# Opening of a four-stage convolution kernel: order of the sample loads, of sample 2's statistics and of the first stack copies

## The reference

```python
x = x + conv(_gn(x))        # stage 0: 3x3, reflect padding; kernel mixed per sample from 3 experts
x = x + conv1(abs(_gn(x)))  # stage 1: 3x3 depthwise, zero padding
x = x + box(_gn(x))         # stage 2: 17x17 mean, zero padding
x = x + mlp(_gn(x))         # stage 3: sum of the 8 neighbours, then 5 pixelwise layers, elu between
```

## Time and profile before

| | |
|---|---|
| median of 3 runs | 767.77 us (767.4 to 771.08) |
| the profiled execution | 776.6 us, its span 774.7 |
| PE, DVE, ACT, POOL busy | 624.3, 611.5, 563.9, 200.6 us |
| DMA | 85.5 MB, mean 110 GB/s; SP's queue 78.6 MB, ACT's 6.3 |
| chain that ended last | PE 36%, DVE 22%, ACT 17%, DMA 8%, issue 8%, SP's queue 6% |
| first layer of round 1 | starts at 137.91 us |

### The profile page before, as it was taken

The page is one execution under the profiler, slowest core; times in us unless marked ns, Lnnn a source line. Parts: engine busy times, 40 slices in busy tenths (PEclk is TensorE's granted clock), DMA queues, the critical chain, the costliest instruction groups (busy, mean ns, idle before and its releaser), DMA issues.

```text
span 774.7 us, 13144 instructions
## 1 busy us (share of the span) xinstructions
PE 624.3 (81%) x4142; PEld 188.2 (24%) x4142; DVE 611.5 (79%) x1100; ACT 563.9 (73%) x1081; POOL 200.6 (26%) x291
## 2 busy tenths in 40 slices
PE   0351845899798999899889988999899789889992
PEld 0211211223222222233223322322232223222220
DVE  1352785598959998989988998879887889769993
ACT  0112110689868998899889988998898968898882
POOL 1302024402541235213521353125300630230000
PEclk9985886899989999999999999999999999999996
DMA  5759499407985739254834574455640560065002
GB/s 98 139 91 178 101 189 211 73 14 146 170 192 97 173 88 206 66 112 107 183 87 109 110 164 107 109 112 132 141 109 3 125 146 1 2 146 125 1 1 54
DMA packets 72865, 85.53 MB, mean 110 GB/s; under 512 B 8674, under 2 KB 58354, under 8 KB 72818
## 3 DMA queue, kind: packets, MB, share of 16 engines
q1 hardware_dynamic: 68096, 78.58, 47.6%
q10 hardware_dynamic: 4722, 6.34, 4.5%
HBM read 9.14 MB, written 8.39 MB: 23 GB/s over the span
## 4 chain that ended last, share of the span: by engine, by line
PE 36%; DVE 22%; ACT 17%; DMA 8%; issue 8%; SPq 6%; POOL 1%; ACTq 1%; DVEq 0%; POOLq 0%
PE pz L756 19%; PE pc L702 8%; ACT u L610 7%; DVE g L991 6%; ACT u L618 6%; PE pc L733 6%; DMA win<-y 5%; DVE u L987 3%; ACT u L615 2%; DVE bn L923 2%; DVE box_sum L1024 2%; DMA xs<-in_x_dram 2%; DVE xs L974 2%; PE po L763 2%; DMA stack<-near_sum 2%
## 5 line engine op out<-in xcount | busy, mean ns | idle before, releaser
L610 ACT ACTIVATE u<-pz 128x512 f32<-128x512 f32 x472 | 275.4, 603 | 93.3 <-PE pz L756 92.7
L756 PE MATMUL pz<-g,wT 64*64 64x512 f32 x1536 | 296.7, 614 | 18.7 <-DVE g L991 15.1
L991 DVE SCALAR_TENSOR_TENSOR g<-u,pz 128x512 f32<-128x512 f32 x384 | 250.3, 681 | 62.1 <-ACT u L618 58.7
L618 ACT ACTIVATE u<-u 128x512 f32<-128x512 f32 x472 | 289.6, 643 | 1.3
L756 PEld LDWEIGHTS pz<-g,wT 64*64 64x64 f32 x1536 | 80.5, 132 | 212.2 <-issue 210.4
L733 PE MATMUL pc<-win,t 64*32 64x512 f32 x1392 | 98.0, 667 | 27.0 <-DMA win<-y 16.0
L702 PE MATMUL pc<-box_sum,box_mat 128*128 128x512 f32 x180 | 90.9, 621 | 12.3 <-DVE box_sum L1024 12.3
L923 DVE BATCH_NORM_STATS2 bn<-xs 128x6 f32<-128x512 f32 (+1 forms) x128 | 82.8, 682 | 22.0 <-DMA xs<-in_x_dram 20.2
L468 POOL TENSOR_TENSOR stat<-stat,con 128x1 f32<-128x1 f32 x32 | 22.5, 704 | 272.9 <-DVE stat L943 272.9
L991 DVE SCALAR_TENSOR_TENSOR g_last<-u,pz 128x512 f32<-128x512 f32 x128 | 82.5, 680 | 9.1 <-ACT u L618 7.1
L756 PE MATMUL pz<-stack,wT 64*64 64x512 f32 x512 | 81.7, 620 | 9.5 <-DMA stack<-near_sum 4.2
(11 more groups left out here) (87 smaller groups left out, 366.6 us busy)
## 6 DMA issues: line engine op xcount, KB each, us to landing
stack<-near_sum SPq DMA_DIRECT2D x90, 192.0 KB, 4.0
win<-y SPq DMA_DIRECT2D x56, 260.0 KB, 4.2
win<-y SPq DMA_DIRECT2D x56, 195.0 KB, 4.3
out_dram<-xs SPq DMA_DIRECT2D x8, 1024.0 KB
stack<-box_sum SPq DMA_DIRECT2D x60, 128.0 KB, 3.8
xs<-in_x_dram SPq DMA_DIRECT2D x7, 1024.0 KB
stack<-near_sum SPq DMA_DIRECT2D x30, 128.0 KB, 3.4
win<-y ACTq DMA_DIRECT2D x8, 260.0 KB, 8.2
```

Of the source, the lines that this page charges most:

```text
L610: act.activation(u[:, m, :], pz[:, m, :], ACT.Relu, scale=-1.0, bias=0.0).then_inc(relu_done, 1)
L618: act.activation(u[:, m, :], u[:, m, :], ACT.Exp, scale=-1.0).then_inc(exp_done, 1)
L756: last = pe.matmul(pz[to, m, :], wT[rows, l, rows], src, start=True, stop=True)
L991: dve.scalar_tensor_tensor(out=elus(l)[:, m, :], in0=u[:, m, :], scalar=-1.0, in1=pz[:, m, :], op0=ALU.add, op1=ALU.max).then_inc(g_writte ...
```

## The change

SP: load 1 becomes one whole load behind w0(0); load 2 goes behind w1(0); in round 1, load 5 goes behind w0(3). The copies of stacks(0, 0) for stack tensors 0 and 1 stay on SP, those for 2 and 3 go to ACT; stacks(0, 1) goes from ACT to SP. `loaded(i)` counts one load per sample. POOL swaps `scales(2, 0)` and `scales(0, 2)`. ACT's `softmax_exp(2)` goes behind its stack copies. PE's `group_sums(2, 0)` goes behind conv0(1), `logits(2)` behind `group_sums(0, 3)`, `group_sums(1, 2)` into round 1 behind conv0(2)'s first pair, and DVE's `group_var(1, 2)` there too. DVE's statistics of sample 2 go behind sample 0's four scans, with the later steps of its routing further down. In `near_first`, `normal3(0, 1)` goes behind the sums of half 0.

```diff
@@ SP's list
             sp.dma_start(tables[2], con_late).then_inc(s_late, 16)
-            load_rows(1, 0, R // 2)
             sp.wait_ge(zeroed, N_ZEROED)
             windows0(sp, 0, (0,), True)
-            load_rows(1, R // 2, R)
-            sp.wait_ge(x_loaded, LOAD * 3)
+            load(1)
+            windows1(sp, 0, (0,), True)
+            sp.wait_ge(x_loaded, loaded(1))
             load(2)
-            windows1(sp, 0, (0,), True)
             sp.wait_ge(conv_mm[0], 2)
             windows0(sp, 1, (0,), True)
             sp.wait_ge(x_loaded, loaded(2))
...
-            stacks(sp, 0, 0)
+            stacks(sp, 0, 0, (0, 1))
+            stacks(sp, 0, 1)
@@ SP, one(t)
-                if first:
-                    sp.wait_ge(x_loaded, loaded(4))
-                    load(5)
                 if has(t + 2):
                     sp.wait_ge(conv_mm[0], 2 * (t + 2))
                     sp.nop(nofuse=True)
                     windows0(sp, t + 2, range(2), True)
+                if first:
+                    sp.wait_ge(x_loaded, loaded(4))
+                    load(5)
@@ POOL's list
-            scales(2, 0)
             scales(0, 2)
+            scales(2, 0)
             scales(1, 1)
@@ ACT's list
             windows0(act, 1, (1,), False)
-            softmax_exp(2)
...
-            stacks(act, 0, 1)
+            stacks(act, 0, 0, (2, 3))
+            softmax_exp(2)
@@ PE, one(t) and its list
+                        if first and at == 0:
+                            group_sums(1, 2)
...
-            group_sums(2, 0)
-            logits(2)
             conv_taps(0, 1, 0, range(3))
             conv_taps(0, 1, 1, range(3))
             group_sums(0, 2)
             conv_taps(1, 0, 0, range(3))
             conv_taps(1, 0, 1, range(3))
+            group_sums(2, 0)
...
-                    group_sums(1, 1)
+                    group_sums(1, 1, (2, 0))
             group_sums(0, 3)
+            logits(2)
             group_sums(3, 0)
             conv_taps(1, 1, 0, range(3))
             conv_taps(1, 1, 1, range(3))
-            group_sums(1, 2)
@@ DVE, near_first
                 normal3(0, 0)
-                normal3(0, 1)
                 dve.wait_ge(y3_edges, 2)
-                dve.wait_ge(y3_written, 2)
+                dve.wait_ge(y3_written, 1)
...
+                normal3(0, 1)
@@ DVE, one(t) and its list
+                        if first and at == 0:
+                            group_var(1, 2)
...
-            stats_of(2, 0, range(Q))
-            merge_stats(2, 0)
             route_out(1)
-            group_var(2, 0)
-            pool_features(2)
-            softmax_in(2)
             evacuate_pair(0, 1, 0)
...
                 box_scan(0, c)
+            stats_of(2, 0, range(Q))
+            merge_stats(2, 0)
             evacuate_pair(1, 0, 0)
             evacuate_pair(1, 0, 1)
             stats_of(1, 1, (0, 2, 1, 3))
             merge_stats(1, 1)
+            group_var(2, 0)
             evacuate(0, 2, 0)
...
             near_first()
-            route_out(2)
+            pool_features(2)
             stats_of(3, 0, range(Q))
+            softmax_in(2)
             merge_stats(3, 0)
             group_var(3, 0)
+            route_out(2)
             evacuate_pair(1, 1, 0)
...
             merge_stats(1, 2)
-            group_var(1, 2)
             rounds(dve, one)
```

More of the change, by code:

```diff
@@ L281, in loaded @@
         def loaded(i):
-            return LOAD if isinstance(i, int) and i == 0 else LOAD * (i + 2)
+            return LOAD * (i + 1)
         def has(i):
@@ L359, in windows1, with stacks @@
                         eng.dma_start(dst, rows).then_inc(win1_in, 16)
-        def stacks(eng, i, h):
+        def stacks(eng, i, h, ms=range(M)):
             eng.wait_ge(near_rows, Q * i + 2 * h + 2)
@@ L369, in stacks @@
             up, down = max(lo, 1), max(lo - 1, 0)
-            for m in range(M):
+            for m in ms:
                 a, b = max(2 * m - 1, 0), min(2 * m + 3, R)
@@ L375, in stacks @@
                 eng.dma_start(stack[m][5 * C:5 * C + bottom, lo:hi], near_sum[2 * C * m:C * b, lo:hi]).then_inc(stack_in[h], 16)
-            eng.dma_start(stack[0][0:C, up:hi], near_sum[7 * C:P, up - 1:hi - 1]).then_inc(stack_in[h], 16)
-            eng.dma_start(stack[3][7 * C:P, down:hi - 1], near_sum[0:C, down + 1:hi]).then_inc(stack_in[h], 16)
+            if 0 in ms:
+                eng.dma_start(stack[0][0:C, up:hi], near_sum[7 * C:P, up - 1:hi - 1]).then_inc(stack_in[h], 16)
+            if 3 in ms:
+                eng.dma_start(stack[3][7 * C:P, down:hi - 1], near_sum[0:C, down + 1:hi]).then_inc(stack_in[h], 16)
         block = ctx.enter_context(nc.Block())
@@ L385, in load @@
                 sp.dma_start(xs[:, bass.ds(i * N, N)].rearrange("p (k w) -> p k w", w=W), xv[i]).then_inc(x_loaded, 16)
-            def load_rows(i, first, end):
-                sp.dma_start(xs[first * C:end * C, i * N:(i + 1) * N].rearrange("p (k w) -> p k w", w=W),
-                             xv[i][first:end]).then_inc(x_loaded, 16)
             load(0)
@@ L544, in _ @@
             spread(pool, 1)
+            scales(0, 2)
             scales(2, 0)
-            scales(0, 2)
             scales(1, 1)
```

## The result

The changed kernel takes 776.3 us (median of 6 runs, 774.74 to 779.2), the kernel before beside it 770.27 (6 runs, 767.4 to 772.32). The ratio is 1.0095, 95% interval 1.0069 to 1.0121: some 7.3 us slower (6.0 by the medians), where +3.3 us, 0.4%, was forecast. The profiled execution took 775.68 us (span 773.8).

What follows compares the result with a forecast made beforehand. The prediction took transfers to bound the opening, and nearly full PE, ACT and DVE the later rounds. Opening +6.3, into round 1 0 and load 5 −3.0 gave +3.3 us: 779.9 profiled, 771.1 as median, range 762 to 777.

Steps and rivals of the forecast that it cites:

- the opening's events: Up to the first layer: load 2 delays w0(1), late statistics delay w0(2), then conv1(1); first layer at 144.2 us.
- 88.9: Opening: landing of w0(1), sample 1's stage-0 windows, from 83.2 + 6.0 − 0.3; bounds 80 to 94 us.
- e: End of conv0(1), the stage-0 convolution of sample 1: 94.1 us before, 97.2 forecast, 3.1 later.
- Rival A: Opening: load 2 uses slots that windows leave; first layer −2.6, total about −7 us, 761; chance 0.20.
- rival B: Opening: w1(1) is through by e + 33, stacks set the start as before; sum 0, 767.9 us; chance 0.20.
- the half load of sample 1: Opening: a half load takes as long as a whole one, at 57 against 106 GB/s; w0(0) 0.3 us sooner.
- its price: Opening: the first layer starts at 144.2 instead of 137.9 us, +6.3.
- into round 1: First layer and round 1: moved sums and variance cost about 1.2 us, quicker matmuls give 1.2 to 1.7; taken as 0.
- Load 5 behind w0(3): Round 1: PE's wait for w0(3) goes, stacks(1,0) land later; gain between 5.7 and 0.9 us, middle −3.0.
- rival C: Start of round 2: the wait for w0(3) turns into one for stacks(1,0); +6.3 + 0 to +1, 774 to 775 us; chance 0.15.

Runs made afterwards that it cites:

- r5: The changed kernel again with no edit, timed against the kernel before: 777.6 us, ratio 1.0103.
- r9: The changed kernel with load 5 moved behind load 4, before round 1: 771.64 us, ratio to the kernel before 1.0020.
- r3: The changed kernel with load 5 put back ahead of w0(3) in round 1: 772.3 us, ratio to the kernel before 1.0021.
- r8: The changed kernel with load 2 behind w0(1) on SP's queue: 770.76 us, ratio to the kernel before 1.0011.
- r12: The changed kernel with load 2 behind w0(1) and load 5 behind load 4: 766.4 us, ratio to the kernel before 0.9955.
- r6: The kernel before with load 5 alone moved behind w0(3): 771.85 us, ratio to the kernel before 1.0040.
- r10: The kernel before with load 5 alone moved behind load 4, before round 1: 768.86 us, ratio to the kernel before 0.9977.
- r4: The kernel before with stack half 0 on two queues, near_first reordered and load 5 behind w0(3): 765.7 us, ratio to the kernel before 0.9963.
- r14: The kernel before, unchanged, profiled in another execution: 770.79 us.
- r15: The kernel before, unchanged, profiled in a further execution: 769.97 us.
- r13: The kernel before, unchanged, profiled once more: 771.86 us.

## Why the prediction was wrong

**Right, with luck: the opening's events.** In the profiled execution w0(1) is held behind load 2 until 89.67 (forecast 88.9); w0(2) is issued at 105.44 (105.7); conv0(1) ends at 94.58 + 2.79 = 97.4 (e = 97.2); conv1(1) starts at 134.70 (e + 37 = 134.2); the first layer at 143.77 with no wait for the stacks (144.2). Rival A (the load hides) falls with 89.67, rival B (w1(1) not held back) with 134.70; the profile names nothing that ends PE's 11.60 us there, and that it is w1(1) is read from SP's queue, which issues its copies until 127.2. But this execution is the latest of the four with this opening: in r5, r9 and r3 conv0(1) starts at 87.2 to 88.0, conv1(1) at 131.0 to 132.7, the first layer at 139.8 to 141.4. And the 88.9 came from two errors that cancel. It was the landing of before, 83.2, plus 6.0 for the load's bytes on engines taken as full. With no load ahead of it w0(1) is there by 76.92 in r8 and ends PE's wait at 77.98 in r12, so the load's place costs 9 to 13 us from an earlier base. It costs them at the issue (12.12 us for one copy), and from 82 to 89 the engines of the changed kernel are not full (0.56, 113 GB/s). PE in r12, then the stretch:
```profile
77.98 4.17 PE L730 MATMUL pc<-win,t 64*32 64x512 f32 x48 [0.60 <-DMA win<-y]
```
```profile
82.00:89.00 7.00, 0.00 (x0) 0.00 (x0) 6.80 (x10) 0.00 (x0) 0.00 (x0) 0.50 0.56 113
```
On the half load of sample 1: the whole load, which in the changed kernel runs between 38 and 46 us, keeps the DMA engines at 0.61 and 105 GB/s, twice the half's rate.
```profile
38.00:46.00 8.00, 7.60 (x96) 2.11 (x80) 2.88 (x5) 0.00 (x0) 0.00 (x0) 1.00 0.61 105
```

**Too high, but within its bounds: its price.** +6.3 was forecast (bounds +2.3 to +7.3), and 143.77 − 137.91 is +5.9. But openings scatter by several us. The mean of the first layer's start is 138.4 over five profiles of before (137.9, 137.2, 137.5, 139.3, 140.2) and 141.5 over four with the changed opening (143.8, 139.8, 141.4, 140.9): +3.0. If r6 and r10 (132.5, 135.7), whose opening is that of before, are counted too, +4.3. Timed with load 5 out of the way on both sides, the changed kernel is 771.64 − 768.86 = 2.8 us above the kernel before. So the term was some 2 to 3.5 us too large.

**Right within its bounds: into round 1, 0 ± 1.5.** With no wait in it, round 1 is 82.5 us in r10 and 81.6 in r9: −0.9.

**Wrong: "Load 5 behind w0(3)", −3.0.** The term was a gain of 5.7 less a loss of 2.7 at stacks(1,0), which is the middle of its bounds. The loss was there, at about this size or above: behind w0(3) instead of out of the way costs 771.85 − 768.86 = 3.0 us in the kernel before, 765.7 − 763.78 = 1.9 with the split stacks (r4 also has near_first reordered), 776.3 − 771.64 = 4.7 in the changed kernel; by the ratios it is 4.9, 3.2 and 5.8. One such difference is uncertain by some 3 us; the three have one sign, and round 1 in the profiles says the same (86.5 for 82.5, 84.8 for 82.2, 85.1 for 81.6). The gain was not there: ahead of w0(3) instead of out of the way costs 0.9, 2.3 and 0.7 us (by the ratios 1.8, 3.2 and 0.1). The 5.7 us had been read from the earlier trace rows, a long wait with the fallen clock behind it. That execution took 776.6, 8.8 above the median of the three runs shown. The prediction took the 8.8 off the sum, but left in it a term that was part of them: against r14 and r15 that execution is 5.8 to 6.6 us longer in all, and 5.4 to 5.7 of these lie in round 1. In r14 and r15 the same wait is 1.98 and 1.95 us, and round 1 is 83.5 and 83.2, 1.0 and 0.7 above r10's 82.5. So the move took away a wait worth one to two us on the average of the timed runs and put in its place one worth 2 to 6. That is rival C (load 5 takes away round 1's gain) in a stronger form: C let the gain come to nothing or to a loss of at most 1. The failed step is thus the 5.7 us of wait and fallen clock, taken from one execution: removing them gained 0.9 us in the kernel before (r10, 1.8 by the ratio).

**The sum again, with what was measured.** Opening and into round 1 together +2.8 as timed (+3.0 to +4.3, less 0.9, by the profiles), load 5's move +2.3 (r6) to +4.0 (changed kernel against r3) by the medians and +3.1 to +5.7 by the ratios: +4 to +9, with the 6.0 and the 7.3 measured inside. The profiles agree once the executions of before are r14 and r15: against these the changed kernel's first layer is 3.6 to 4.4 us later, its round 1 is 1.6 to 1.8 longer, and the rest differs by −1.0 to +0.4, together +5.0 to +5.8.

What stays open: why an execution of before takes the long or the short wait. The long ones came with the earlier first layer (137.2 to 137.9, the short ones 139.3 and 140.2): PE came to the wait at 207.4 to 208.5 in the long cases and at 209.1 and 209.7 in the short ones, and went on at 210.3 to 212.5 in all five. That is five executions, and no run set out to test it. Nor is it settled why the move costs more in the changed kernel than in the other two; the differences lie within what these timings can tell. And the other parts of the change (load 1 in one piece, the late statistics of sample 2, the order in `near_first`) were not tried one by one: r12 has them beside r11, with load 2 behind w0(1), and is 2.6 us above it, which these timings hardly tell from none.

**A version that beats both.** r11, the kernel before with stack half 0 on two queues and load 5 behind load 4: 763.78 us, ratio 0.9922 (0.9895 to 0.9949) to before, 12.5 us below the changed kernel. Its round 1 has neither wait:
```profile
133.52 2.85 PE L758 MATMUL pz<-stack,wT 64*64 64x512 f32 x16
...
215.76 1.95 PE L758 MATMUL pz<-stack,wT 64*64 64x512 f32 x16
```

## What to carry to other kernels

A term read from one profiled execution may be there in some executions and not in others, and the very wait that one wants to remove can be what made that execution long. Compare its time with the median of the timed runs (here 776.6 with 770), and take two or three more profiles before the term goes into a sum; being near the median is not enough, for r13 had the long wait 0.2% above it. An event that comes out as forecast in one profile needs the same care. A load that collides with urgent copies isn't helped by going behind them if the next urgent copies are then behind it: look in the table of stretches for a place where the DMA engines do nothing. Split a transfer over two queues where an engine waits for its landing, and expect nothing of it where something else is later.

## What the runs showed of the hardware

Two things were not expected. In the five executions of the kernel before, the same wait for the same copies has two outcomes with nothing between: near 2 us, after which 32 matmuls take 1.95 us at a granted clock of 1.00, or 3 to 4 us, after which they take 3.67 at 0.50 and the round is 3.7 to 5.7 us longer. The length alone doesn't decide it: r13 waited 2.96 us and went on at 0.50, while r5 waited 3.47 for the stacks and ran the next 16 matmuls in 2.16 at 1.00, and r6 waited 2.98 and ran them in 2.84 at 0.74 on average. And what a load does to copies behind it on the queue shows in their issue, not only in their transfer: five copies took 14.96 us to issue right behind a load, 4.56 at the same place without it.
